# First graph layer of a one-core graph network: tile-by-tile waits, an adjacency product with its last node tile last, a bias product in eight passes, basis groups in pairs

## The reference, cut to what matters

```python
h = jnp.maximum(_layernorm(x), 0.0)
A = zeros((512, 512)).at[src, dst].add(edge_weight)          # 16384 edges
deg = A.sum(axis=1); dinv = where(deg > 0, deg ** -0.5, 0)
A = dinv[:, None] * A * dinv[None, :]
for l in range(2):
    h = A @ h
    h = h @ W_gcn[l] + b_gcn[l]
    h = leaky_relu(h @ W_mlp[l] + b_mlp[l], 0.01)
x = x + h
```

## Time and profile before

| | us |
|---|---|
| median of 3 runs | 868.13 |
| lowest and highest run | 865.55, 871.05 |
| the profiled execution, its own time | 865.51 |
| the span of its trace | 864.0 |
| PE busy in the span | 830.5 |
| DVE busy | 562.7 |
| ACT busy | 397.5 |
| POOL busy | 232.5 |
| mean granted TensorE clock | 0.994 |

### The profile page before, as it was taken

One profiled execution on the slowest core, in us unless ns is written; L12 is line 12 of the kernel. 1 busy time (PEld: TensorE's weight loads), 2 busy tenths in 40 slices (PEclk: granted clock), 3 DMA queues, 4 the chain that ended last, 5 costly groups with the idle time before them and its releaser, 6 DMA issues. The chain is left out here.

```text
span 864.0 us, 13175 instructions
## 1 busy us (share of the span) xinstructions
PE 830.5 (96%) x4222; PEld 631.3 (73%) x4223; DVE 562.7 (65%) x1228; ACT 397.5 (46%) x646; POOL 232.5 (27%) x258
## 2 busy tenths in 40 slices
PE   6999889999799999999999999999999999999998
PEld 3666546767578778777697777787786976688786
DVE  7999998649958666576667575774776666720210
ACT  4999984234446512355433365233663235531200
POOL 4000033208432224402236022334013424422200
PEclk9999999999899999999999999999999999999999
DMA  8989966534224735533727329255348388020101
GB/s 186 211 212 239 263 156 165 145 98 114 97 68 93 205 89 160 145 105 112 181 87 178 96 52 233 74 156 141 99 147 194 106 218 219 13 98 1 49 13 37
DMA packets 59350, 113.44 MB, mean 131 GB/s; under 512 B 4372, under 2 KB 4936, under 8 KB 59292
## 3 DMA queue, kind: packets, MB, share of 16 engines
q1 hardware_dynamic: 42108, 79.00, 38.4%
q10 hardware_dynamic: 17184, 33.69, 11.9%
HBM read 105.33 MB, written 7.34 MB: 130 GB/s over the span
## 5 line engine op out<-in xcount | busy, mean ns | idle before, releaser
L683 POOL TENSOR_TENSOR wl<-wraw,wh 128x512 fp32r<-128x512 f32 x140 | 181.1, 1327 | 358.9 <-ACT wh L757 346.4
L688 POOL TENSOR_TENSOR rstd<-ve,half 128x1 f32<-128x1 f32 x48 | 26.3, 550 | 211.2 <-DVE ve L1146 210.9
L1803 PE MATMUL ring<-ohs,ohd 128*128 128x512 f32 x312 | 78.0, 401 | 2.8 <-DVE ohs L1317 2.8
L1803 PEld LDWEIGHTS ring<-ohs,ohd 128*128 128x128 f32 x312 | 57.8, 190 | 27.4 <-issue 14.8
L1295 DVE SCALAR_TENSOR_TENSOR ohd<-iota,dstT,vals 128x256 fp32r x156 | 69.5, 483 | 2.9 <-issue 1.8
L757 ACT ACTIVATE wh<-wraw 128x2048 fp32r<-128x2048 f32 x35 | 66.8, 1910 | 8.1 <-DMA wraw<-in_L_gnn_root 4.5
L782 ACT ACTIVATE yT_h<-ring 128x512 fp32r<-128x512 f32 x32 | 19.0, 598 | 97.9 <-PE ring L1719 97.9
L806 ACT ACTIVATE ohs<-iota,minus_srcT 128x512 fp32r<-128x512 f32 x78 | 52.2, 713 | 9.0 <-issue 6.4
L1730 PE MATMUL mix_ps<-quad,att_shift 120*32 120x512 f32 x384 | 50.1, 603 | 0.0
L1701 PE MATMUL ring<-yT_h,wh 128*128 128x512 f32 x128 | 49.8, 389 | 0.0
L1701 PE MATMUL ring<-yT_l,wh 128*128 128x512 f32 x128 | 49.8, 389 | 0.0
(11 more groups left out here) (384 smaller groups left out, 2149.6 us busy)
## 6 DMA issues: line engine op xcount, KB each, us to landing
quad<-in_L_gnn_basis SPq DMA_DIRECT2D x60, 960.0 KB, 9.9
wraw<-in_L_gnn_m_w ACTq DMA_DIRECT2D x8, 1024.0 KB, 10.0
mix_scratch<-mixed SPq DMA_DIRECT2D x128, 32.0 KB
wraw<-in_L_gnn_wv ACTq DMA_DIRECT2D x4, 1024.0 KB, 5.1
wraw<-in_L_gnn_wq ACTq DMA_DIRECT2D x4, 1024.0 KB, 5.3
wraw<-in_L_gnn_wk ACTq DMA_DIRECT2D x4, 1024.0 KB, 5.3
wraw<-in_L_gnn_wo ACTq DMA_DIRECT2D x4, 1024.0 KB, 5.4
wraw<-mix_scratch ACTq DMA_DIRECT2D x4, 1024.0 KB, 5.7
```

The costliest lines, as they stand in the source:

```text
L683: last = g.tensor_tensor(wl[s][:, k, :], wraw[s][:, k, :], wh[s][:, k, :].bitcast(F32), ALU.subtract)
L1803: last = te.matmul(ring[:, banks[b], :], ohd[:, s, b, :], ohs[:, s, :], start=False, stop=False)
```

## The change

- `taken` on the last tile ahead of a stage becomes a `taken` per k step within the stage's first tile (`tile0_by_rows`). This holds for `Y`, `H0`, `U` and `H1`.
- `G` keeps four tiles open: it first does k steps 0 to 2 of all four (36 passes), then waits for the last tile of `H0`, then does k step 3 of each (12 passes).
- `c0` takes one four-column weight `bg` (two columns high, two low) against `wh` and `wl`: 8 passes in place of 12, into four rows; one selector row is added to another so that the bias matmul sums the four rows.
- `z2` moves behind `H0` on PE, in `n0_names` and on DVE (`stack_conditioning` behind the four `H0` tiles).
- The six single mixing groups become three pairs: ahead of `c0`, ahead of `H0` and ahead of `H1`. None is left after `c0`, `z2`, `H0` or `G`.

The core of the diff:

```diff
-                   + [("Y", t) for t in range(4)] + ["z2"] + [("H", 0, t) for t in range(4)] + [("G", t) for t in range(4)]
+                   + [("Y", t) for t in range(4)] + [("H", 0, t) for t in range(4)] + ["z2"] + [("G", t) for t in range(4)]
...
+                v.tensor_tensor(sel[:, 0, :], f(sel[:, 0, :]), f(sel[:, 1, :]), ALU.add)
                 v.tensor_copy(gwh[:], gates).then_inc(sel_step, 1)
-                v.tensor_copy(bgh[:], bias).then_inc(sel_step, 1)
+                v.tensor_copy(bg[:, :, 0:2], bias).then_inc(sel_step, 1)
...
-                v.tensor_tensor(bgl[:], bias, f(bgh[:]), ALU.subtract).then_inc(tile_taken, 1)
+                v.tensor_tensor(bg[:, :, 2:4], bias, f(bg[:, :, 0:2]), ALU.subtract).then_inc(tile_taken, 1)
...
-                v.tensor_tensor(bias_raw[0:2, :], bias_raw[0:2, :], bank(n0, "c0")[0:2, :], ALU.add).then_inc(tile_taken, 1)
+                v.tensor_tensor(bias_raw[0:4, :], bias_raw[0:4, :], bank(n0, "c0")[0:4, :], ALU.add).then_inc(tile_taken, 1)
...
-            stack_conditioning()            (ahead of the H0 tiles)
...
+            stack_conditioning()            (behind them)
             split_cond(0, 0)
...
+            def tile0_by_rows(name, bias, lh, ll, m, rh, rl, source):
+                out = begin(n0, B, name)
+                if bias is not None:
+                    te.matmul(out, bias[0], bias[1], start=True, stop=False)
+                for k in range(KT):
+                    if m == 0:
+                        taken(n0, B, source(k))
+                    for n, (l, r) in enumerate(product(lh, ll, k, m, rh, rl)):
+                        last = te.matmul(out, l, r, start=bias is None and k + n == 0, stop=k == KT - 1 and n == 2)
+                last.then_inc(tile_ready, 1)
...
-            mix_groups(1)
+            mix_groups(2)
             s = slot(1)
             pe.wait_ge(weight_lo, 2)
             pe.wait_ge(sel_step, 8)
-            multiply(begin(n0, B, "c0")[0:2, :], [... three(bgh[:, k, :], bgl[:, k, :], wh[s][:, k, :], wl[s][:, k, :])])
-            mix_groups(1)
-            taken(n0, B, ("V", KT - 1))
+            for k in range(KT):
+                te.matmul(out, bg[:, k, :], wh[s][:, k, :], start=k == 0, stop=False)
+                last = te.matmul(out, bg[:, k, :], wl[s][:, k, :], start=False, stop=k == KT - 1)
             for t in range(NT):
-                tile0(("Y", t), products(hb_h[1], hb_l[1], t, wh[s], wl[s]))
+                tile0_by_rows(("Y", t), None, hb_h[1], hb_l[1], t, wh[s], wl[s], lambda k: ("V", k))
+            mix_groups(2)
+            pe.wait_ge(deg_step, 2 + 3 * NT)
+            pe.wait_ge(sel_step, 10)
+            for t in range(NT):
+                tile0_by_rows(("H", 0, t), bias_to_rows(0, bias_rows), An_h, An_l, t, hb_h[0], hb_l[0], lambda k: ("Y", k))
             pe.wait_ge(emb_step, 7)
             te.matmul(begin(n0, B, "z2"), fw2[:], sil[0][:], start=True, stop=True).then_inc(tile_ready, 1)
-            mix_groups(1)
...
-            mix_groups(1)
+            outs = []
+            for m in range(KT):
+                outs.append(begin(n0, B, ("G", m)))
+                for k in range(KT - 1):
+                    if m == 0:
+                        taken(n0, B, ("H", 0, k))
+                    for n, (l, r) in enumerate(product(hb_h[1], hb_l[1], k, m, An_h, An_l)):
+                        te.matmul(outs[m], l, r, start=k + n == 0, stop=False)
             taken(n0, B, ("H", 0, NT - 1))
             for m in range(KT):
-                tile0(("G", m), products(hb_h[1], hb_l[1], m, An_h, An_l))
-            mix_groups(1)
+                for n, (l, r) in enumerate(product(hb_h[1], hb_l[1], KT - 1, m, An_h, An_l)):
+                    last = te.matmul(outs[m], l, r, start=False, stop=n == 2)
+                last.then_inc(tile_ready, 1)
             counts(0)
             counts(1)
...
             s = slot(3)
-            mix_groups(1)
+            mix_groups(2)
```

More of the change, by code:

```diff
@@ L181, in program @@
         gwl = sb("gwl", [P, 2, KT, 2], F32R)
-        bgh = sb("bgh", [P, KT, 2], F32R)
-        bgl = sb("bgl", [P, KT, 2], F32R)
+        bg = sb("bg", [P, KT, 4], F32R)
         bias_columns = sb("bias_columns", [P, len(COLUMN_BIASES), BLOCKS * KT])
@@ L1397, in _ @@
                 low_of(("Y", t), hb_l[0][:, t, :], hb_h[0][:, t, :])
-            stack_conditioning()
             def counts(j):
@@ L1417, in _ @@
                 v.tensor_tensor(CT[0][:, t, :], Csum[:, t, :], CT[1][:, t, :], ALU.subtract).then_inc(ct_ready, 1)
+            stack_conditioning()
             split_cond(0, 0)
@@ L1854, in _, with product @@
             B = n0.base
-            def tile0(name, pairs):
-                multiply(begin(n0, B, name), pairs).then_inc(tile_ready, 1)
             def counts(j):
                 transposes(begin(n0, B, ("C", j)), [cols(Csum, m, j) for m in range(NT)]).then_inc(tile_ready, 1)
-            def products(lh, ll, m, rh, rl):
-                return [p for k in range(KT) for p in three(cols(lh, k, m), cols(ll, k, m), rh[:, k, :], rl[:, k, :])]
+            def product(lh, ll, k, m, rh, rl):
+                return three(cols(lh, k, m), cols(ll, k, m), rh[:, k, :], rl[:, k, :])
+            def tile0_by_rows(name, bias, lh, ll, m, rh, rl, source):
[8 more added lines that the diff above has]
+                last.then_inc(tile_ready, 1)
             for t in range(NT):
@@ L1901, in _ @@
             pe.wait_ge(sel_step, 8)
-            multiply(begin(n0, B, "c0")[0:2, :], [p for k in range(KT) for p in three(bgh[:, k, :], bgl[:, k, :], wh[s][:, k, :], wl[s][:, k, :])]
-                     ).then_inc(tile_ready, 1)
-            mix_groups(1)
-            taken(n0, B, ("V", KT - 1))
-            for t in range(NT):
-                tile0(("Y", t), products(hb_h[1], hb_l[1], t, wh[s], wl[s]))
+            out = begin(n0, B, "c0")[0:4, :]
+            for k in range(KT):
+                te.matmul(out, bg[:, k, :], wh[s][:, k, :], start=k == 0, stop=False)
+                last = te.matmul(out, bg[:, k, :], wl[s][:, k, :], start=False, stop=k == KT - 1)
@@ L1924, in _ @@
             pe.wait_ge(weight_lo, 3)
-            taken(n0, B, ("G", KT - 1))
             for m in range(KT):
-                tile0(("U", m), [bias_to_columns(2, bias_rows, m)] + products(wh[s], wl[s], m, hb_h[0], hb_l[0]))
+                tile0_by_rows(("U", m), bias_to_columns(2, bias_rows, m), wh[s], wl[s], m, hb_h[0], hb_l[0], lambda k: ("G", k))
                 if m + 2 < NT:
@@ L1930, in _ @@
             s = slot(3)
-            mix_groups(1)
+            mix_groups(2)
             pe.wait_ge(weight_lo, 4)
-            taken(n0, B, ("U", KT - 1))
             for t in range(NT):
-                tile0(("H", 1, t), [bias_to_rows(3, bias_rows)] + products(hb_h[1], hb_l[1], t, wh[s], wl[s]))
+                tile0_by_rows(("H", 1, t), bias_to_rows(3, bias_rows), hb_h[1], hb_l[1], t, wh[s], wl[s], lambda k: ("U", k))
             assert not early
```

## The result

| | us |
|---|---|
| before, median of 6 runs | 868.64 (865.55 to 872.08) |
| after, median of 6 runs | 863.60 (862.32 to 864.95) |
| ratio | 0.9938, 95% interval 0.9915 to 0.9961 |
| profiled execution after, its own time | 864.37 |
| span of its trace | 862.8 |

The change saves 5.0 us, 0.6%; the interval allows 3.4 to 7.4. It is within the 1% of "no change" and in the range on record (857.3 to 866.8), 2.0 us above the forecast of 861.6 and short of the forecast gain of 6.5.

A forecast was written before the change was run, and what follows sets the result against it. PE, 96% busy, was taken to bound the kernel, with DVE's path behind `U`. Six terms summed to -6.55 us at `U`'s end; 868.1 - 6.5 gave 861.6 us (chance 0.60), range 857.3 to 866.8.

The forecast's parts named there:

- 1, 2: At `c0`: four passes fewer, -0.92 us; the groups after `z1` and `c0` become a pair, -0.23 us.
- 3: Between `Y` and `H0`: the wait for `silu`, `z2` and one group give way to a pair, -0.82 us.
- 4: Between `H0` and `G`: a group and 1.87 us idle give way to `z2`, -1.88 us.
- 5, 6: `G` all at full clock, -1.71 us; between `G` and `U` one group goes and the transposes stay, -0.99 us.
- Open tiles and new waits: In `G`, open banks and some 20 new waits cost 0, at most 0.03 us each, 0.6 in all.
- The slow case: Rival *Slower*: four open tiles break PE's stream, all of `G` gets 1.2 GHz, 870.9 us; chance 0.03.
- Basis loads: Loads for moved groups arrive in time, 3 us to spare for set 5; rival of a late load, chance 0.01.
- PE's 0.33 us: Behind `U` a pair takes 1.95 us where PE had 1.62; costs nothing, as DVE takes the first `H1` tile later.
- 6.5 us earlier: Behind `H1`: PE's start of the next layer follows DVE and comes 6.5 us earlier.
- the prediction's own sign of being wrong: A gain at `U`'s end that is smaller at 260 us would show the forecast wrong.
- the rival at 863.3: The slow clock in `G` was in few executions, so the gain is only 4.8 us; chance 0.20.
- More: Second slow stretch, around 227 us, may fall away too, 1.7 us: -8.2 in all, 859.9; chance 0.16.

The follow-up runs named there:

- look_before: The kernel before, unchanged, profiled in another execution: 868.76 us.
- before_early: The kernel before with the fourth and fifth weights' high parts (ACT) and low parts (GpSimd) made earlier: 865.53 us, ratio 0.9951 to the kernel before.
- after_closed: The changed kernel with `G` as before the change (one wait for the last `H0` tile, tiles one after another): 865.67 us median of 10.
- look_closed: after_closed again, unchanged, in another execution: 868.66 us.

## Why the prediction was right, point by point

| step of the sum | worked out | measured (start to start in the two traces) |
|---|---|---|
| 1, 2: first mixing group ahead of `c0` to `Y` | -0.92 - 0.23 = -1.15 | 3.71 against 4.86: -1.15 |
| 3: `Y` to `H0` | -0.82 | 12.83 against 13.78: -0.95 |
| 4: `H0` to `G` | -1.88 | 13.15 against 15.05: -1.90 |
| 5, 6: `G` to `U` | -1.71 - 0.99 = -2.70 | 11.82 against 14.54: -2.72 |
| sum | -6.55 | -6.72 |

- **Passes and pairs.** The eight four-column passes stand 0.23 us apart and a pair takes 1.86 us (148.90 to 150.76). Both as taken.
- **Open tiles and new waits** cost nothing: 48 passes of `G` and the transposes behind them take 11.82 us. The slow case, with 1.2 GHz over all of `G`, did not come; all of it was granted 2.4 GHz, 1.00 in the window at 180. The case of the Trainium skill that the prediction cites beside it ("TensorE: Matmul & The Clock Gate", A second HAM failure mode: psum-queue depth-cycling), in which PE idles briefly between groups of matmuls while it cycles through banks, did not show here.
- **Basis loads.** The pair ahead of `H0` follows `Y` without idle time. Right, though the working has a slip: the fourth group of set 5 stood at 175.26 before, so by the prediction's own 160.2 it is used 15 us earlier, not 13.
- **Behind `U`.** PE's 0.33 us did cost nothing: `H1` is 0.37 us longer behind `U` on PE (14.82 against 14.45), and DVE doesn't wait for it. The step that failed is the one that lets PE's start of the next layer follow DVE "6.5 us earlier": it takes DVE's chain from the last low part of `U` on to move as a block. Its start moved by 6.7 us, but the four masks grew from 3.59 to 4.96 us, +1.37, because GpSimd's work came only partly with it. 0.37 us came back in the additions to `x`. So the term was 5.7 and not 6.55 at the last `H1` tile, and still 5.7 at the weight product of the next layer that waits for DVE (240.53 before, 239.22 after; 96.98 against 91.28 us from `z1`). That is the prediction's own sign of being wrong, a gain at `U`'s end that is smaller further on. I had treated the durations of DVE's rows as fixed, and read no row of GpSimd beside them.
- **The clock in `G`.** I left open whether its slow rows belong to the execution. A slow stretch was there in all five traces that have an idle time ahead of `G` (before, look_before, before_early, after_closed, look_closed) and in none of the seven without it. So the -1.71, taken from one execution, was there in every trace; when the forecast was made, that was open, and in this it had luck. What differs between executions is the length, 1.3 or 2.8 us of cost in one kernel, and above all the stretches elsewhere, behind the degrees. The Trainium skill ("TensorE: Matmul & The Clock Gate", Part 1: The HAM clock gate) tells that the number of slow matmuls at the start of one kernel differs from run to run; these traces show such a difference in the middle of one. So the rival at 863.3, whose time is the closest, was close for another reason than its own.
- **The second slow stretch**, on which the rival *More* rested, stayed: from 226 to 233 us before, from 224 to 231 us after, with a mean granted clock of 0.51 over both windows, and behind 3.98 us of idle time after the change.
- **The profiled execution and the median.** I put the 2.6 us between them down to the spread of the runs. The traces show what it is: the first trace is the only one of ten without a slow stretch behind the degrees, which costs 1.6 to 3.2 us.

Counted from `z1` to the end of the span, the change is worth 5.6 and 6.4 us in the two pairs of traces; the medians say 5.0 with 3.4 to 7.4. The difference is within what the stretches ahead of `z1` shuffle. Of the 2.0 us by which the time lies above the forecast, 0.9 is the term on DVE, 0.5 is the median before (868.64, where the forecast started from 868.13), and the other 0.6 is within the spread of the runs.

## What to carry to other kernels

When a stretch is moved earlier, ask of the bounding engine not only what it waits for but what runs beside it: a row's duration is that of its neighbourhood. Where a product needs the last tile of the stage before, keeping its outputs open and taking that tile last hides a whole hand-over, and here it took the slow clock behind the idle time away with it (3.5 us on PE for one edit, 2.6 in the median). Lay traces over each other at a fixed instruction before subtracting, since slow stretches ahead of the changed code can be as large as the effect.

## What the runs showed of the hardware

- DVE operations whose operands and result lie in SBUF slow down while GpSimd works: 0.68 us for a 128x512 mask with GpSimd idle, up to 1.8 beside its subtractions; 0.42 against 1.51 us for a copy of the same size. Operations that read PSUM kept 0.68 us beside GpSimd work (the counts, 192 to 202 us after the change). GpSimd slows down too: its four subtractions took 5.05 us beside those counts, and 6.1 to 6.9 beside the operations from SBUF to SBUF. A mask that was already running when GpSimd began kept 0.69 us, and GpSimd's 128x128 addition beside it took 0.88 in place of 0.46 (204.79 and 204.92 us after the change). The mechanism behind it was not tried.
- TensorE can be granted 1.2 GHz without idle time just before. Behind the start of 32 records of two columns, 3.6 us in one block, a slow stretch set in within the block or right behind it in nine of ten traces, while PE was busy throughout; in four blocks of 0.95 us among full passes, in none of two.
